# One input of each rotation instruction moved to PSUM, and one room for radial results instead of two

## The reference

```python
x = _layernorm(x + mean_of_neighbours(x, src, dst))
# message layer
R = relu(edge_weight[:, None] @ w1 + b1) @ w2 + b2          # 384 radial weights of an edge
Y = spherical_harmonics(edge_attr_3)                        # 1, 3 and 5 values
Fj = x[src]                                                 # 8 scalars, 8 vectors
acc += norm * einsum('euv,ef,evi,ofi->euo', R_k, Y_f, F_b, C)   # for each pair of l and each lf
out = zeros.at[dst].add(msg)
x = _layernorm(x + out)
```

## Time and profile before

| | |
|---|---|
| median of the runs | 3802.33 us |
| profiled execution, its own time | 3812.7 us |
| its span (first to last instruction) | 3811.0 us |
| first layer and nodes, to the first gather of the message layer | 1594.6 us |
| gathers of the message layer, first to last issue | 1594.6 to 3620.1 us |
| rest of the message layer and nodes | 3620.1 to 3811.0 us |
| mean granted TensorE clock | 0.919 |
| busy: TensorE, VectorE, ScalarE, POOL | 3141.5, 2725.8, 2088.1, 2812.7 us |

### The profile page before, as it was taken

One profiled execution on the slowest core, in us unless ns is written; L12 is line 12 of the kernel. 1 busy time (PEld: TensorE's weight loads), 2 busy tenths in 40 slices (PEclk: granted clock), 3 DMA queues, 4 the chain that ended last, 5 costly groups with the idle time before them and its releaser, 6 DMA issues.

```text
span 3811.0 us, 56548 instructions
## 1 busy us (share of the span) xinstructions
PE 3141.5 (82%) x17216; PEld 1983.1 (52%) x17216; DVE 2725.8 (72%) x3385; ACT 2088.1 (55%) x2391; POOL 2812.7 (74%) x2915
## 2 busy tenths in 40 slices
PE   3999999999999883268888888888888888888863
PEld 2898989898989772223333333333333333333332
DVE  4787778787878684457777777767767776776755
ACT  4787777786877650045555545555555554555520
POOL 7777777777777776677777777777777777777726
PEclk9999999999999995589999999999999999999975
DMA  4122121122211211122222222222222222222211
GB/s 99 40 54 43 40 54 43 50 44 54 44 50 43 50 48 29 38 47 52 62 52 61 62 52 62 61 52 60 53 62 52 62 62 52 62 52 62 56 27 25
DMA packets 201360, 197.69 MB, mean 52 GB/s; under 512 B 60626, under 2 KB 149812, under 8 KB 201014
## 3 DMA queue, kind: packets, MB, share of 16 engines
q1 hardware_dynamic: 108436, 149.13, 13.8%
q0 software_dynamic: 92832, 47.72, 8.5%
HBM read 134.02 MB, written 62.59 MB: 52 GB/s over the span
## 4 chain that ended last, share of the span: by engine, by line
PE 51%; POOL 19%; issue 12%; DVE 8%; DMA 6%; ACT 2%; DVEq 1%; SPq 1%; POOLq 0%; ACTq 0%
PE ps_r L952 19%; POOL got L686 14%; PE ps_m L952 10%; PE ps_r L1016 7%; PE ps_m L1028 6%; PE ps_r L1003 6%; DMA got<-x_d,idx 5%; POOL ngot L666 4%; DVE prod_room L1701 3%; DVE unit L1701 2%; PE ps_r L936 1%; PE ps_m L1039 1%; ACT hot_s L737 1%; ACT hot_s L740 1%; DVE ps_m L1408 1%
## 5 line engine op out<-in xcount | busy, mean ns | idle before, releaser
L686 POOL DMA_INDIRECT got<-x_d,idx x1564 | 1528.9, 978 | 505.2 <-issue 470.5
L641 POOL DMA_INDIRECT deep_room<-in_x_dram,idx_deep x657 | 631.3, 961 | 200.2 <-PE ps_r L952 83.8
L952 PE MATMUL ps_r<-x_hi,hot_s 128*128 128x448 f32 x1974 | 738.3, 374 | 45.3 <-ACT hot_s L740 45.3
L952 PE MATMUL ps_r<-x_lo,hot_s 128*128 128x448 f32 x1974 | 730.0, 370 | 0.0
L815 ACT ACTIVATE count_room<-ps_r,bias_col 128x1024 f32<-128x1024 f32 x294 | 327.6, 1114 | 704.3 <-PE ps_r L1016 687.9
L1016 PE MATMUL ps_r<-hid,wc 64*128 64x512 f32 x2352 | 642.1, 626 | 2.0 <-DVE bias_col L1388 2.0
L737 ACT ACTIVATE hot_s<-rows,minus_row 128x512 fp32r<-128x512 f16 (+1 forms) x658 | 449.0, 764 | 233.6 <-PE ps_m L952 198.2
L1003 PE MATMUL ps_r<-feat_hi,spread_by 64*128 64x512 f32 x1176 | 310.6, 525 | 313.2 <-DVE prod_room L1701 166.0
L1003 PEld LDWEIGHTS ps_r<-feat_hi,spread_by 64*128 64x128 f32 x1176 | 115.0, 192 | 702.7 <-DVE prod_room L1701 259.4
L1679 DVE TENSOR_TENSOR part<-got,frame 128x384 f32<-128x384 f32 x294 | 191.6, 680 | 396.6 <-DMA got<-x_d,idx 396.6
L952 PEld LDWEIGHTS ps_r<-x_hi,hot_s 128*128 128x128 f32 x1974 | 377.7, 191 | 75.9 <-issue 46.6
(11 more groups left out here) (212 smaller groups left out, 5728.9 us busy)
## 6 DMA issues: line engine op xcount, KB each, us to landing
hid<-weight_t SPq DMA_DIRECT2D x196, 256.0 KB
run_d<-runs_t SPq DMA_DIRECT2D x194, 256.0 KB
got<-x_d,idx POOLq DMA_INDIRECT x1564
deep_room<-in_x_dram,idx_deep POOLq DMA_INDIRECT x657
rows<-code_d SPq DMA_DIRECT2D x47, 160.0 KB
frame_d<-x_sb SPq DMA_DIRECT2D x7, 1008.0 KB, 4.8
frame<-frame_d SPq DMA_DIRECT2D x98, 72.0 KB
frame_b<-frame_d SPq DMA_DIRECT2D x98, 72.0 KB
```

The lines of the kernel that those rows point to most:

```text
L641: pool.indirect_dma_start(got_deep[k][:, t, :], None, x, bass.IndirectOffsetOnAxis(ap=idx_deep[q][:, k * T + t:k * T + t + 1], axis=0)).th ...
L686: pool.indirect_dma_start(got[k][:, t, :], None, x1_d, bass.IndirectOffsetOnAxis(ap=idx[k][:, t:t + 1], axis=0)).then_inc(got2_landed[k], 16)
L952: mm = pe.matmul(found[BANK_OF[k][g]], hot_s[k][:, a, g, :], part[:, a * LN * D:(a + 1) * LN * D], start=(a == 0 and n == 0), stop=(a == B ...
```

## The change

Radial results get one room (banks 0 and 1). Step s now waits for the copy of step s - 1. The two banks that come free take two things. Bank 2 holds `rotating`: the first product of the rotation and its running sum. Bank 3 holds `frame_in`: a copy of the batch's frame, which ScalarE makes (`keep_frame`) ahead of the third radial copy of a batch, when the load has landed and the rotation before is done. The three products read the frame from `frame_in`, and VectorE waits for that copy instead of for the load. The second and third product are still written to SBUF.

```diff
-        radial_unit = [banks[:, 2 * u:2 * u + 2, :] for u in range(2)]
+        radial_unit = banks[:, 0:2, :]
+        rotating = banks[:, 2, 0:T * 3 * MUL].rearrange("p (t i v) -> p t i v", t=T, i=3)
+        frame_in = banks[:, 3, 0:T * 9].rearrange("p (t c a) -> p t c a", c=3, a=3)
...
+            def keep_frame(b, k):
+                act.wait_ge(frame_loaded[k], 8 * (b - k + 2))
+                if not isinstance(b, int) or b > 0:
+                    act.wait_ge(rotated_in, b)
+                act.copy(frame_in, frame[k][:, :, :, :]).then_inc(frame_kept, 1)
...
                         keep_feat_lo(b + 1, 1 - k)
+                    if not last:
+                        keep_frame(b + 2, k)
+                    if more:
                         keep_radial(b + 1, 2)
...
-                if not isinstance(b, int) or STEPS_R * b + step > 1:
-                    pe.wait_ge(radial_kept, STEPS_R * b + step - 1)
+                if not isinstance(b, int) or STEPS_R * b + step > 0:
+                    pe.wait_ge(radial_kept, STEPS_R * b + step)
...
-                    dve.wait_ge(frame_loaded[k], 8 * (b - k + 2))
+                    dve.wait_ge(frame_kept, b + 1)
...
-                    s.mark(dve.tensor_tensor(part[:, c], spread(f1[:, :, :, c], 2, 3),
-                                             spread(frame[k][:, :, c, :], 3, MUL), ALU.mult))
+                    s.mark(dve.tensor_tensor(rotating if c == 0 else part[:, c], spread(f1[:, :, :, c], 2, 3),
+                                             spread(frame_in[:, :, c, :], 3, MUL), ALU.mult))
...
-                s.mark(dve.tensor_tensor(part[:, 0], part[:, 0], part[:, 1], ALU.add))
+                s.mark(dve.tensor_tensor(rotating, rotating, part[:, 1], ALU.add))
...
-                dve.tensor_tensor(got[k][:, :, MUL:D].rearrange("p t (a v) -> p t a v", a=3), part[:, 0], part[:, 2],
+                dve.tensor_tensor(got[k][:, :, MUL:D].rearrange("p t (a v) -> p t a v", a=3), rotating, part[:, 2],
```

More of the change, by code:

```diff
@@ L335, in build_program @@
         frame_loaded = pair("frame_loaded")
+        frame_kept = sem("frame_kept")
         got2_landed = pair("got2_landed")
@@ L814, in keep_radial @@
                     act.wait_ge(multiplied, PRODUCTS * (b - 1) + G4 * p + LAST_USE_OF_KEPT[c])
-                act.activation(kept[p][c], radial_unit[step % 2], ACT.Identity, bias=bias_col[:, c:c + 1]
+                act.activation(kept[p][c], radial_unit, ACT.Identity, bias=bias_col[:, c:c + 1]
                                ).then_inc(radial_kept, 1)
@@ L871, in _ @@
             act.wait_ge(bias_kept, 1)
+            keep_frame(0, 0)
             next_idx(0, 0)
@@ L876, in _ @@
             keep_feat_lo(0, 0)
+            keep_frame(1, 1)
             keep_radial(0, 2)
@@ L1011, in radial @@
                     pe.wait_ge(hid_ready, b + 1)
-                if not isinstance(b, int) or STEPS_R * b + step > 1:
-                    pe.wait_ge(radial_kept, STEPS_R * b + step - 1)
+                if not isinstance(b, int) or STEPS_R * b + step > 0:
+                    pe.wait_ge(radial_kept, STEPS_R * b + step)
                 for h in range(2):
                     rows = slice(h * H, h * H + H)
-                    mm = pe.matmul(radial_unit[step % 2][:, h, :], wc[rows, c * P:(c + 1) * P],
+                    mm = pe.matmul(radial_unit[:, h, :], wc[rows, c * P:(c + 1) * P],
                                    hid[k][rows, p * G4 * P:(p + 1) * G4 * P], start=True, stop=True)
```

## The result

The changed kernel takes 3760.6 us (median, 3758.79 to 3762.86 us) against 3803.6 us for the kernel before, measured with it. The ratio is 0.9888, 95% interval 0.9870 to 0.9905: 1.1% faster, 43 us. The forecast was 3751 us. The profiled execution takes 3759.97 us, its span is 3758.2 us, and the granted TensorE clock is 0.929.

What follows compares the result with a forecast made beforehand. The prediction took POOL's gather issue rate to bound the message layer. From the profiled 3812.7 us, -52.7 (slow issues) and +1 (tail), copy and room 0, gave 3761.0; from the median, 3751 us, range 3742 to 3762 (3778 with half the gain).

Steps and rivals of the forecast that it cites:

- POOL sets the message layer: Message layer: the issue rate of POOL's 1564 gathers, one per 1.2485 us, sets 2025.5 us of 3811.
- The slow issues: POOL's gathers: 164 issues over 1.0 us instead of 0.944 us, nearly all beside rotation instructions with two SBUF inputs.
- The size, -52.7 us: POOL's queue: time saved when the five rotation instructions each read one input from PSUM.
- the same step gives 3750.6: Final sum: the change from 3812.7 to 3761.0 us, applied to the 3802.3 us median, gives 3750.6 us.
- late frame copies: ScalarE's frame copy: a few might wait for the frame's load; the forecast's own range, 3742 to 3762 us, allowed for them.
- The frame copy: ScalarE, ahead of the third radial result: 0.31 us a batch, hidden, so 0; uncovered 30 us.
- The single room: TensorE's radial matmuls: 0.4 to 0.65 us lost a batch, hidden; as rival (c), becoming the bound, chance 7%.
- The cover: VectorE's 4.05 us a batch of waiting for gathers hides added waits; 2.9 us left after the change.
- The tail, +1 us: After the last gather, two and a half batches paced by VectorE and TensorE lose 0.5 to 1.6 us.
- The lead of the transposes: Time from a buffer's transposes to its next gather: shortest lead shrinks from 5.3 to 4.1 us.
- L1679 at 550 to 680 ns: Rotation's three part products on VectorE, 677 ns before: predicted to take 550 to 680 ns after the change.
- The rule of the Trainium skill: VectorE against GpSimd: a tensor_tensor does not stall a GpSimd-issued DMA, so no gain; basis of rival (a), chance 5%.

Runs made afterwards that it cites:

- the kernels with twelve gathers: Changed kernel and kernel before, each with 12 gathers a batch instead of 16 from the third batch on: 3523.7 us with the change, 3493.8 us without.
- each half of the change: Changed kernel with the frame read from SBUF: 3772.9 us (ratio 0.9913); changed kernel with the running sum in SBUF: 3783.8 us (0.9941).
- one operand at another place: Changed kernel plus two unused 896-element VectorE products a batch: both inputs in SBUF 3823.2 us, one input in PSUM 3764.3 us.
- the second look at the same kernel: Kernel before, unchanged, profiled once more: median 3805.1 us (ratio 0.9995), profiled execution 3805.83 us, 140 slow issues instead of 164.
- the room and the copy alone: Changed kernel with all five rotation instructions on SBUF operands as before, keeping the single room and frame copy: 3797.0 us, ratio 0.9983.

## Why the prediction was right, and where it was off

1. **POOL sets the message layer**: right. The table shows it, the kernels with twelve gathers show that slow issues stop costing time when POOL is not the bound, and with 13 pauses left, 1563 beats of 1.2485 us, 1951.4 us, and 21.4 us make the measured 1972.85 us. The forecast said 1972 to 1975.
2. **The slow issues are the rotation's two SBUF inputs**: right. The mean is 944 ns, as forecast; each half of the change removes its own, and one operand at another place makes or unmakes 59 us.
3. **The size, -52.7 us**: right for the execution that it was read from. The sum against it gave 3761.0 us, and the changed kernel's profiled execution took 3759.97. **Wrong was the step from there to the median**: "the same step gives 3750.6". The 10.4 us by which that execution lay over the median were not a constant on top but mostly more slow issues: 52.7 us of them, where the second look at the same kernel had 42.9. An ordinary execution had only some 43 us to give. The term was over-sized by 10 us for the median; all of the miss of 9.6 us is in it. The measured 3760.6 us lie inside the range by 1.4 us only, and the room above was left for late frame copies, which did not come: that it holds this miss is luck. A check of the size was at hand: at random phase, five instructions that read for 0.53 us (three) and 0.40 us (two) would cost (3 x 0.53^2 + 2 x 0.40^2)/(2 x 1.2485) x 98 = 46 us. But that this comes near 43 is partly luck too: the same formula gives 33 and 13 us for the two halves, which measured 12.2 and 21.3. The phase is not random, since the first part product of a batch starts when a gather lands.
4. **The frame copy**: 296 ns, forecast 0.31 us, hidden. The load never made it late: ScalarE stands idle ahead of the copy once in 98 times, for 0.8 us, and that wait is for another thing.
5. **The single room**: forecast 0.4 to 0.65 us a batch and hidden. TensorE's new waits are 0.46 us, and of that 0.33 us lie on the round once the cover is gone. The mechanism was right, and the measured loss lies at the lower end of the forecast.
6. **The cover**: too large in the forecast. It took VectorE's whole wait for the gather (4.05 us) as spare time and left 2.9 us. The kernel with twelve gathers shows a round of 17.75 us, so at 20.1 us a batch some 2.4 us are spare (an estimate, as the granted clock was 0.99 there and 0.96 in the changed kernel; the 2.1 us of the added products with one input in PSUM did fit under it). VectorE's waits for TensorE ahead of its products are 1.66 us a batch in the changed kernel and 2.78 us with twelve gathers: take the one wait away and part of it comes back as the other. The batch became 0.54 us shorter by the change, and of that 0.25 us came off the wait for the gather (4.05 to 3.80) and 0.29 us off these waits for TensorE (1.95 to 1.66), so the first did not fall into the range of 2.5 to 3.7 that I gave.
7. **The tail, +1 us**: it is 190.9 us before and 190.0 us after (3811.0 - 3620.1 and 3758.2 - 3568.25), so nothing can be seen of it.
8. **The lead of the transposes**: forecast 4.1 us at its shortest, measured 4.41 us (one batch at the start; else 5.2 us or more). It never held POOL up.
9. **L1679 at 550 to 680 ns**: the part products stay at 677 ns, and the one that writes to PSUM takes 714 ns. That they are slower than others of 384 elements has nothing to do with the second SBUF input; the strided input is left as a cause and was not tried.

**The rule of the Trainium skill** (SBUF — State Buffer, "Who interferes with whom") keeps its first half: two SBUF inputs on VectorE contend with what reads SBUF on GpSimd, and the later one waits. A gather issue takes its indices from `idx`, a tile in SBUF; that this reading is what waits is likely and not shown. Its inference, that making descriptors needs the write interface and a tensor_tensor so does not stall a GpSimd-issued DMA, does not hold here: the gather issues waited for up to 0.92 us behind products with two SBUF inputs, also where these wrote to PSUM. The prediction went too far where it said that the trace agrees with a wait until the first is through: the issue at 2658.88 us was 0.11 us behind its sum and lasted 0.31 us over the floor, so it was let go 0.42 us from the start of an instruction of 0.55 us.

## What to carry to other kernels

Where a queue never idles and its instructions come in two lengths, lay its timeline beside that of each other engine and count the long ones by what had just started there: the cause and the whole gain can be read before a line is changed. Take the saving from the execution whose loss you counted, and ask of the median how much of that loss it has: a loss that hangs on phase differs from run to run. And measure the cover of an added wait by taking the bound away (fewer gathers), not by one engine's idle time; here some 2.4 us were left where the idle time said 3.8.

## What the runs showed of the hardware

- A gather issue on POOL that starts behind such a VectorE instruction is let go before the instruction ends: 0.42 us from its start for 384 contiguous elements (of 0.55 us), 0.96 us for 896 (of 1.085 us), and for a copy of 896 0.49 us (of 0.62 us). By these lengths it waits for the reading; that is inferred. An issue that is under way isn't held, nor was any that started less than 0.039 us behind; at 0.04 us both occur.
- A float32 copy from SBUF to SBUF holds POOL as two inputs do, though it has one: 67 of 67 issues.
- A change that leaves POOL's work alone can still move the time by 7 us (the room and the copy alone, ratio 0.9983), since fewer issues meet the rotation.
- POOL pauses for 1.5 to 1.8 us more than usual exactly every 112 gather issues (13 times in 1564, in every kernel in which its queue was never empty). In the kernel with two products of two SBUF inputs three of the 13 pauses are 0.8 to 0.9 us instead, each behind an issue that was held for 0.8 us: a hold and a pause overlap. In the kernel with twelve gathers, where POOL waits each batch anyway, such a pause can't be told from its waits. Its cause stays open.
